# Routing tokens to experts batch by batch during attention, with the experts' token lists written to DRAM by indirect DMAs

## The reference: cross attention, then a mixture of experts

```python
x = x + attention(query=layernorm(x), key=ctx, value=ctx)   # softmax(Q K^T / sqrt(32)) V, then @ Wo.T + bo
flat = layernorm(x).reshape(4096, 512)
logits = flat @ router_weight.T + router_bias               # 8 experts
topk_vals, topk_idx = top_k(softmax(logits), 2)
gate, up = split(flat @ gate_up_proj[e] + gate_up_bias[e])  # per expert e, 512 -> 2 x 512
gate = minimum(gate, 7); up = clip(up, -7, 7)
act = (up + 1) * gate * sigmoid(1.702 * gate)
x = x + sum over the 2 best experts of w_e * (act @ down_proj[e] + down_bias[e])
```

## Time and profile before

| | |
|---|---|
| median of three runs | 1759.33 us (1756.08 to 1760.47) |
| the profiled execution | 1756.44 us, of which the span is 1754.7 us |
| mean granted TensorE clock | 0.965 of full speed |
| TensorE busy | 1617.4 us (92%) |
| VectorE busy | 1246.5 us (71%) |
| GpSimd busy | 801.6 us (46%) |
| ScalarE busy | 659.0 us (38%) |
| attention | until about 971 us |
| routing | 971 to 1019 us |
| experts | 1019 us to the end |

### The profile page before, as it was taken

The page is one execution under the profiler, slowest core; times in us unless marked ns, Lnnn a source line. Parts: engine busy times, 40 slices in busy tenths (PEclk is TensorE's granted clock), DMA queues, the critical chain, the costliest instruction groups (busy, mean ns, idle before and its releaser), DMA issues. The chain is left out here.

```text
span 1754.7 us, 30046 instructions
## 1 busy us (share of the span) xinstructions
PE 1617.4 (92%) x9637; PEld 1189.2 (68%) x9637; DVE 1246.5 (71%) x2223; ACT 659.0 (38%) x1265; POOL 801.6 (46%) x619
## 2 busy tenths in 40 slices
PE   5889999999999999999987269999999999999995
PEld 3545555555565655556533269999999998999994
DVE  4675777777777767776664867777878778777873
ACT  3354544545445354454441033223333233222320
POOL 3364656556565655556564022333343433434332
PEclk9999999999999999999998569999999999999998
DMA  6342343434334334333311421324443353324321
GB/s 215 81 122 66 104 111 83 130 89 110 108 92 113 103 93 120 96 100 95 89 52 60 159 74 62 98 86 159 162 153 115 94 206 112 105 79 148 113 79 66
DMA packets 98804, 188.69 MB, mean 108 GB/s; under 512 B 26320, under 2 KB 27344, under 8 KB 98640
## 3 DMA queue, kind: packets, MB, share of 16 engines
q1 hardware_dynamic: 79408, 123.99, 25.0%
q0 software_dynamic: 19232, 62.73, 11.2%
HBM read 204.19 MB, written 37.36 MB: 138 GB/s over the span
## 5 line engine op out<-in xcount | busy, mean ns | idle before, releaser
L677 DVE TENSOR_REDUCE negmax<-max_ps 128x2 f32<-128x1024 f32 x256 | 312.4, 1220 | 203.7 <-PE max_ps L446 203.4
L566 ACT ACTIVATE pt<-work 128x512 f32<-128x512 f32 x512 | 278.4, 594 | 242.2 <-PE work L458 228.8
L760 POOL TENSOR_TENSOR acc<-acc,pt 128x1024 f32<-128x1024 f32 x128 | 303.8, 2377 | 121.8 <-ACT pt L566 121.8
L1295 PE MATMUL gu_ps<-xgT_hi,wg_hi 128*128 128x256 f32 x1248 | 355.3, 285 | 0.0
L1295 PE MATMUL gu_ps<-xgT_hi,wg_lo 128*128 128x256 f32 x1248 | 352.0, 282 | 0.0
L1295 PE MATMUL gu_ps<-xgT_lo,wg_hi 128*128 128x256 f32 x1248 | 351.8, 282 | 0.0
L757 POOL TENSOR_TENSOR acc<-pt 128x1024 f32<-128x1024 f32 x64 | 152.9, 2391 | 248.9 <-PE work L478 181.1
L1295 PEld LDWEIGHTS gu_ps<-xgT_lo,wg_hi 128*128 128x128 f32 x1248 | 235.8, 189 | 0.1
L1295 PEld LDWEIGHTS gu_ps<-xgT_hi,wg_hi 128*128 128x128 f32 x1248 | 235.7, 189 | 0.1
L1295 PEld LDWEIGHTS gu_ps<-xgT_hi,wg_lo 128*128 128x128 f32 x1248 | 235.6, 189 | 0.0
L1556 POOL DMA_INDIRECT out<-acc,idx x78 | 77.5, 994 | 325.0 <-DVE acc L1450 319.0
(11 more groups left out here) (201 smaller groups left out, 2803.0 us busy)
## 6 DMA issues: line engine op xcount, KB each, us to landing
raw_g<-w_gate_up SPq DMA_DIRECT2D x39, 2048.0 KB
raw_d<-w_down SPq DMA_DIRECT2D x39, 1024.0 KB
ks<-k_hi SPq DMA_DIRECT2D x252, 64.0 KB, 2.0
qs<-q_hi SPq DMA_DIRECT2D x252, 64.0 KB, 2.0
bd<-b_down SPq DMA_DIRECT2D x39, 256.0 KB
x_in<-x SPq DMA_DIRECT2D x32, 256.0 KB, 3.1
ctxT_raw<-ctx_t SPq DMA_DIRECT2D x32, 256.0 KB, 3.9
x<-x SPq DMA_DIRECT2D x32, 256.0 KB, 3.0
```

The lines of the kernel that those rows point to most:

```text
L566: e.activation(pt[k % 2][:, h, :], in_work("exp", u, k, h)[:, :], ACT.Exp, scale=scale).then_inc(exped.sem, 1)
L677: e.tensor_reduce(negmax[:, u % 2, n:n + 2], max_ps[:, :, :], AX.X, ALU.max, negate=True).then_inc(maxed.sem, 1)
L760: e.tensor_tensor(acc[:, heads, :], acc[:, heads, :], pt[k % 2][:, heads, :], ALU.add).then_inc(added.sem, 1)
L1295: ins = e.matmul(gu_ps[n % GU_BANKS][:, part, :], wg[s][pw][:, k, cols], xgT[s][px][:, k, :], start=(k == 0 and m == 0), stop=(k == KD - 1 ...
```

## The change

The routing of a tile no longer waits for all 32.

- The 32 tiles are cut into nine groups: six of the four tiles of a batch, then two of three and one of two. A group's logits, masks and shares stand in one of two halves of small buffers.
- For batches 0 to 5 the group's work has keys in ORDER, in the second to fourth unit of the batch after the next: `best 0` and `best 1` (the two best experts, VectorE) in rounds 2 and 3 of the second unit, `soft` (the exp, ScalarE) in round 4, `share` (VectorE; SP stores the shares) in round 5, `rank` (two accumulating products on TensorE, over the group's masks and the counts of all tiles before it) in round 2 of the third unit, `place` (VectorE) in round 3, and `list` in rounds 2 and 3 of the fourth.
- `list` is new: for each of two experts per token and each tile one indirect DMA of GpSimd writes the 128 token numbers of that tile, 4 bytes each, to their places in a table in DRAM, `token_list`, which has 32 rows of 128 places per expert and 78 spare rows, and is cleared once at the start of the program.
- The last three groups follow at the end: the group of tiles 24 to 26 in step 32, tiles 27 to 29 and 30, 31 in step 33; the four list DMAs of the last group stand in the routing stage.
- The routing stage keeps the counts, the experts of the tiles and these small steps at the end. The one-hot tables and their 64 products are gone. Instead VectorE computes for each of the 78 slots the row of `token_list` where it begins, GpSimd gathers these 78 rows of 512 bytes once all lists have landed, TensorE transposes them, and VectorE copies them.
- Constants (iota, part, tri, ones) are made on GpSimd at the start of the program and turned into floats by VectorE before the first group. The experts' stage waits for nine stores of shares instead of one.

```diff
+def route_groups(n_tiles, batch):
+    last = n_tiles - 2 * batch
+    return [(n, batch) for n in range(0, last, batch)] + [(last, batch - 1), (last + batch - 1, batch - 1), (last + 2 * batch - 2, 2)]
...
+def list_tile(e, token_list, listed, pos, token, n):
+    places = token_list.rearrange("r (q a) -> (r q) a", a=1)
+    for s in range(TOP_K):
+        at = bass.IndirectOffsetOnAxis(ap=pos[:, s, n:n + 1].bitcast(U32), axis=0)
+        e.indirect_dma_start(out=places, out_offset=at, in_=token[:, n:n + 1], in_offset=None).then_inc(listed, 16)
...
+            for r, lag, *keys in ((2, 9, ("best", 0)), (3, 9, ("best", 1)), (4, 9, ("soft",)), (5, 9, ("share",)), (2, 10, ("rank",)), (3, 10, ("place",)),
+                                  (2, 11, ("list", 0), ("list", 1)), (3, 11, ("list", 2), ("list", 3))):
+                g, odd = divmod(s - lag, T)
+                if g in groups[:-3] and not odd:
+                    at(r, *[(kind, g, *what) for kind, *what in keys])
...
+                at(1, ("best", g, 0))
+                at(2, ("best", g, 1), ("soft", g), ("rank", g))
+                at(3, ("place", g))
+                at(4, ("share", g))
+            if s == units[-1] + 2:
+                at(0, *[("list", g, t) for t in range(GROUPS[g][1])])
+                g += 1
+                at(1, ("best", g, 0), ("best", g, 1), ("soft", g))
+                at(2, ("rank", g), ("place", g), *[("list", g, t) for t in range(GROUPS[g][1])])
+                at(3, ("best", g + 1, 0), ("best", g + 1, 1), ("soft", g + 1), ("rank", g + 1), ("share", g), ("place", g + 1), ("share", g + 1))
             if s - 1 in units[:-1]:
                 for t in range(T):
                     at(4 + t, ("norm", s - 1, t))
...
+            def rank_tokens(g):
+                to, slots = take("rank", g), slots_of(g)
+                cols = slice(0, GROUPS[g][1] * E)
+                e.wait_ge(before_made.sem, before_made[g])
+                e.matmul(to[:, cols], tri[:, :], hots[:, slots, :].rearrange("p t e -> p (t e)"), start=True, stop=False)
+                e.matmul(to[:, cols], ones_b[:, :], before[:, slots, :].rearrange("p t e -> p (t e)"), start=False, stop=True).then_inc(ranked.sem, 1)
...
+            def soften(g):
+                e.wait_ge(expo_made.sem, expo_made[g])
+                e.activation(expo[:, slots_of(g), :], expo[:, slots_of(g), :], ACT.Exp).then_inc(softened.sem, 1)
...
+            def best_experts(g, s):
+                slots, n = slots_of(g), GROUPS[g][1]
+                e_of = lambda a: a.unsqueeze(2).to_broadcast([P, n, E])
+                t_of = lambda a: a.unsqueeze(1).to_broadcast([P, n, E])
+                source = masked if s else logits
+                if s == 0:
+                    e.wait_ge(logits_out.sem, logits_out[sum(GROUPS[g]) - 1])
+                last()
+                then(e.tensor_reduce(best[:, s, slots], source[:, slots, :], AX.X, ALU.max))
+                last()
+                then(e.tensor_tensor(scratch[:, slots, :], source[:, slots, :], e_of(best[:, s, slots]), ALU.is_equal))
+                last()
+                then(e.tensor_tensor(scratch[:, slots, :], scratch[:, slots, :], t_of(expert_less[:, :]), ALU.mult))
+                last()
+                then(e.tensor_reduce(pick[:, slots], scratch[:, slots, :], AX.X, ALU.min))
+                last()
+                then(e.tensor_tensor(hot[s][:, slots, :], t_of(expert_less[:, :]), e_of(pick[:, slots]), ALU.is_equal))
+                last()
+                if s == 0:
+                    then(e.scalar_tensor_tensor(out=masked[:, slots, :], in0=hot[0][:, slots, :], scalar=-1e30, in1=logits[:, slots, :],
+                                                op0=ALU.mult, op1=ALU.add))
+                    return
+                then(e.tensor_tensor(hots[:, slots, :], hot[0][:, slots, :], hot[1][:, slots, :], ALU.add))
+                e.tensor_tensor(expo[:, slots, :], logits[:, slots, :], e_of(best[:, 0, slots]), ALU.subtract).then_inc(expo_made.sem, 1)
+                if g and slots.start == 0:
+                    then(e.tensor_copy(before[:, 0, :], before[:, SLOTS, :]))
+                for t in range(slots.start, slots.stop):
+                    last()
+                    ins = e.tensor_tensor(before[:, t + 1, :], before[:, t, :], hots[:, t, :], ALU.add)
...
+            def share(g):
+                slots, n = slots_of(g), GROUPS[g][1]
+                e.wait_ge(softened.sem, softened[g])
+                if g in groups[1:-1]:
+                    e.wait_ge(w_stored, 16 * g)
+                then(e.tensor_reduce(exp_sum[:, slots], expo[:, slots, :], AX.X, ALU.add))
+                then(e.tensor_tensor(weight[:, weights_of(g), :], expo[:, slots, :], hots[:, slots, :], ALU.mult))
+                last()
+                then(e.reciprocal(inv_sum[:, slots], exp_sum[:, slots]))
+                last()
+                e.tensor_tensor(weight[:, weights_of(g), :], weight[:, weights_of(g), :], inv_sum[:, slots].unsqueeze(2).to_broadcast([P, n, E]),
+                                ALU.mult).then_inc(weight_made.sem, 1)
+            def place_tokens(g):
+                slots, n = slots_of(g), GROUPS[g][1]
+                e.wait_ge(ranked.sem, ranked[g])
+                then(e.tensor_tensor(scratch[:, slots, :], in_work("rank", g)[:, 0:n * E].rearrange("p (t e) -> p t e", e=E),
+                                     base[:, :].unsqueeze(1).to_broadcast([P, n, E]), ALU.add))
+                for s in range(TOP_K):
+                    last()
+                    then(e.tensor_tensor(hot[s][:, slots, :], hot[s][:, slots, :], scratch[:, slots, :], ALU.mult))
+                for s in range(TOP_K):
+                    last()
+                    then(e.tensor_reduce(pos_f[:, s, slots], hot[s][:, slots, :], AX.X, ALU.add))
+                last()
+                e.tensor_copy(pos[:, :, tiles_of(g)], pos_f[:, :, slots]).then_inc(pos_made.sem, 1)
             for kind, *what in ORDER:
...
+                elif kind == "list":
+                    g, t = what
+                    if what == [0, 0]:
+                        e.wait_ge(s_cleared, 16)
+                    e.wait_ge(pos_made.sem, pos_made[g])
+                    list_tile(e, token_list, listed, pos, token, GROUPS[g][0] + t)
...
             for kind, *what in ORDER:
                 if kind in "kq" and what[1] == 1:
...
+                elif kind == "share":
+                    g, = what
+                    e.wait_ge(weight_made.sem, weight_made[g])
+                    e.dma_start(w_rows[:, tiles_of(g), :], weight[:, weights_of(g), :]).then_inc(w_stored, 16)
...
-            flat_pos = pos[:, :, :].rearrange("p s t -> p (s t)")
...
-            for q in range(NQ):
...
-                then(e.tensor_tensor(row_hot[:, some, :], iota_b[:, :].unsqueeze(1).to_broadcast([P, n_some, P]),
...
-                then(e.tensor_tensor(col_hot[:, some, 0, :], col_hot[:, some, 1, :],
...
-            e.wait_ge(listed, 1)
-            then(e.tensor_copy(low[:, :], list_ps[:, SLOTS:]))
-            last()
-            then(e.scalar_tensor_tensor(out=token_1[:, :], in0=list_ps[:, 0:SLOTS], scalar=float(P), in1=low[:, :],
-                                        op0=ALU.mult, op1=ALU.add), "token_1")
+            then(e.tensor_scalar(slot_hot[:, :], iota[:, 0:E], slot_expert[:, 0:1], None, ALU.is_equal))
+            last()
+            then(e.tensor_tensor(slot_hot[:, :], slot_hot[:, :], start[:, :], ALU.mult))
+            then(e.scalar_tensor_tensor(out=slot_row[:, :], in0=slot_expert[:, :], scalar=float(NT), in1=part[:, 0:1], op0=ALU.mult, op1=ALU.add))
...
+            then(e.tensor_reduce(slot_start[:, :], slot_hot[:, :], AX.X, ALU.add))
...
+            then(e.scalar_tensor_tensor(out=slot_row[:, :], in0=slot_start[:, :], scalar=-float(SUB), in1=slot_row[:, :], op0=ALU.mult, op1=ALU.add))
+            last()
+            then(e.tensor_copy(row_i[:, :], slot_row[:, :]), "rows")
...
+            e.wait_ge(turned, 1)
+            then(e.tensor_copy(token_1[:, :], list_ps[:, :]), "token_1")
...
-            for n in range(KT):
...
-                ins = e.matmul(list_ps[:, :], row_hot[:, n, :], col_hot[:, n, :, :].rearrange("p a c -> p (a c)"),
-                               start=(n == 0), stop=(n == KT - 1))
-            ins.then_inc(listed, 1)
+            e.matmul(count_ps[:, :], ones_b[:, :], before[:, before.shape[1] - 1, :], start=True, stop=True).then_inc(counted, 1)
+            e.wait_ge(columns_in, 16)
+            e.transpose(list_ps[:, :], columns[:, :], ident[0:SLOTS, 0:SLOTS]).then_inc(turned, 1)
...
+        def on_pool(e):
+            e.memset(ones_e[:, :], 1.0).then_inc(consts_made, 1)
+            e.memset(ones_row[:, :], 1.0).then_inc(consts_made, 1)
+            first_tile, n = groups[-1]
+            for t in range(n):
+                list_tile(e, token_list, listed, pos, token, first_tile + t)
+            e.wait_ge(vec, at["rows"])
```

(3 more changed lines are left out.)

300 lines of the change are left out of this document (137 added, 163 removed).

## The result

| | before | after |
|---|---|---|
| median of four runs | 1759.9 us (1756.08 to 1760.69) | 1811.55 us (1809.31 to 1815.18) |
| ratio after to before, 95% interval | | 1.0301 (1.0285 to 1.0318) |
| profiled execution, span | 1756.44, 1754.7 us | 1809.48, 1807.8 us |
| mean granted TensorE clock | 0.965 | 0.956 |

What follows compares the result with a forecast made beforehand. TensorE, busy 291.80 of 300 us in attention, and the 48.9 us routing hole were taken to bound the kernel. Terms -21 + 27 + 2 + 7 + 6 + 1 = +22 gave a median of 1781 us, range 1752 to 1796.

Steps and rivals of the forecast that it cites:

- VectorE in attention, +27: Second units: new VectorE steps wait out GpSimd's adds on the shared port and delay TensorE; +27 us, bounds 0 and 40.
- Rival (1): Attention: VectorE's bursts slip past GpSimd's adds, so the 27 us fall away; 1754 us, 18% chance.
- Rank, +2: Attention: the ranking's two small matmuls per group take 0.3 us each time on TensorE; +2 us.
- GpSimd in attention, +7: Fourth units: eight scatters delay the add and, through ScalarE's exp, TensorE by 1.4 us in five groups; +7, bounds 4 and 14.
- Last unit, +6 and +1: End of attention: lists end 6.5 us late without slack, +6; logits of tiles 27 to 31 pass between new steps, +1.
- Routing stage, -21: Last logits to first index: first index 21.9 us earlier, 0.9 given back for overlap; -21 us, bounds -26 and -15.
- rival (5): Routing stage: the list's gather lies behind 6.3 MB of weights, landing after 7 us instead of 3; 1785 us, no chance given.
- (4): Rival: 4-byte scatters take longer than row scatters, each 0.25 us more costing 12 in attention, 4 in the stage; 1797, 7%.
- (3): Rival: only each best 1's first add is met, lists cost nothing till the last unit; +4, about 1761 us, 10%.
- A batch takes 6 to 7 us more: Sign in attention: each batch takes 6 to 7 us longer than in the kernel before.
- The exp behind them waits for acc: Sign in the fourth unit: ScalarE's exp behind eight list DMAs, 1.3 us apart, waits for GpSimd's add.
- The hole falls to about 27: Sign: last logits to first index falls from 48.9 to about 27 us; staying above 35 means the forecast is wrong.

Runs made afterwards that it cites:

- split_best: The change with best 1 cut in two, the second half one unit later, and the keys after it moved; 1820.21 us, 1.0364 of the kernel before.
- gap64: The change with the places of the table 64 bytes apart instead of 4, still 4 bytes written to each; 1801.07 us, 1.0267 of the kernel before.
- no_lists: The change without the list scatters and the wait for them, so all experts work on token 0; 1753.14 us, 0.9975 of the kernel before.
- gap64_late: gap64_spread with the six scatters of the last group but one moved behind the end of the attention block; 1775.79 us, 1.0097 of the kernel before.
- full64: The change with places 64 bytes apart and all 64 bytes written by each scatter; 1802.7 us, 1.0266 of the kernel before.
- gap64_spread: gap64 with four scatters of a batch in the fourth unit and four in the next; 1771.06 us, 1.0066 of the kernel before.
- gap16_spread: gap64_spread with places 16 bytes apart instead of 64; 1765.26 us, 1.0042 of the kernel before.
- gap16_split: gap16_spread with best 1 split over two units, lists one unit later and rank right ahead of place; 1750.36 us, 0.9955 of the kernel before.
- gap16_late: gap16_split with six scatters moved behind the attention block's end, and SP waiting for all lists before the weights; 1748.65 us, 0.9944 of the kernel before.
- gap16_drain: gap16_split with GpSimd waiting for the scatters issued so far to land before the attention block ends; 1752.72 us, 0.9962 of the kernel before.
- near_split: gap16_split's order with the change's own table, places 4 bytes apart; 1772.62 us, 1.0084 of the kernel before.

## Why the prediction was wrong, step by step

**What bounds the kernel.** Right. TensorE had no time to give: the last logits come 56.3 us later than before, and that is the sum of what single places lost (46.8 from unit 10 to 31, 12.4 in the tail, less 2.9 at the start); nothing was won back in between.

**VectorE in attention, +27; measured +18.8.** The mechanism was right and shown: the blocked steps end with GpSimd's add, split_best takes the loss to 1.3. Mis-sized was how many groups meet a second add. I took four at 5.5 and two at 2.6; measured are 6.0, 2.0, 2.4, 2.0, 2.2 and 4.2, and only the first is seen to meet one. I had written that the second block is missed if the chain is 0.3 us faster, and took the worse side. Part of the two large ones is the clock, which I had left out. Behind the waits of the first group, TensorE (busy 4.84 of the 7.2 us ahead) was granted 0.50 for 6.8 us:

```profile
315.20:322.00 6.80, 5.81 (x20) 2.90 (x21) 6.60 (x10) 1.61 (x3) 2.35 (x1) 0.50 0.36 88
```

and the sixth group loses 4.2 to 4.3 in the four runs whose clock is at 0.50 for 3.4 us there (the change, gap64, no_lists, gap64_late) and 2.6 in the three without (full64, gap64_spread, gap16_spread). Rival (1), that the bursts slip past the adds, is refuted by the row of 2.03 us. **Rank, +2**: 1.2 with place, right.

**GpSimd in attention, +7; measured +26.8.** This step failed, in what it let the scatters delay. I let the add start 4.7 us late, and it does so by 4.3 in gap64 (737.81 at a lag of 27.7, against 705.85); I let nothing wait but the exponential of 710.68, which does need that add, and brought 1.4 us of it to TensorE. In the runs the loss stands before that exponential, at the maximum of round 4: eight scatters in a row make results of TensorE 3.8 us late for their readers, and gap64 loses 3.4 to 4.8 in each of five batches, gap64_spread nothing. How they do that is open. The remaining 7.8 us (26.8 - 19.0), 6.1 of them in the first batch, go with the q stacks of 13.6 us and the fall of the clock behind them (gap64 has the stacks at 2.0), a price of which the trace of before had no row, and which I did not list among the unknowns: I asked what a scatter costs GpSimd, not what it costs the DMA queues.

**Last unit, +6 and +1; measured +12.4.** I counted 6.5 us of delay, and the first add is 5.9 us late against the other engines (968.49, against 918.83 + 43.8). What I left out is what TensorE does after such a wait. Stretches of the change and of before at the same work:

```profile
965.00:970.00 5.00, 1.42 (x13) 0.58 (x5) 3.33 (x6) 0.00 (x0) 4.37 (x4) 1.00 0.02 0
970.00:975.00 5.00, 3.11 (x4) 1.46 (x5) 0.00 (x0) 2.66 (x5) 5.00 (x3) 0.55 0.81 34
975.00:980.00 5.00, 5.00 (x24) 1.99 (x23) 0.00 (x0) 1.36 (x3) 4.97 (x3) 0.76 0.19 20
```

```profile
921.00:926.00 5.00, 5.00 (x32) 2.23 (x28) 3.15 (x6) 3.73 (x7) 5.00 (x4) 1.00 0.18 54
```

After 3.6 of 5 us without work the granted clock is 0.55 and 0.76 in the next two stretches, so most of the first and about half of the second ran at the lower of its two levels (1.2 GHz), where it had been 1.00 (2.4 GHz). What this costs was not measured by itself. no_lists and gap16_split, in which the wait is gone, have tails of 1.3 and 1.1 (gap16_late and gap16_drain, of the same order, 3.1 and 3.8).

**Routing stage, -21; measured -3.1.** The VectorE part was right: no_lists has a hole of 23.3 us, 25.6 less than before, at my lower bound. What failed is the price of the scatters at the memory: 9.76 us of landing where I took 2.3 (bounds 1.5 and 3.5), and 11.50 at the block's end where I took 0.3. I had taken the landing from a scatter of whole rows, whose places lie 2 KB apart. That row holds only for places that are apart: gap64 measured 2.05. The gather of the rows landed 5.0 us after its issue ended (6.0 after it began) where I took 3.0, beside the weights (2 to 7 was its range, and rival (5) its name). Together the three add 20.7 us to the forecast; the hole is 18.8 longer than forecast, so the rest of it came out 2 shorter. By the Trainium skill (DMA: Bandwidth & Descriptors, Anatomy of one DMA) the fixed cost of 2.0 us would have given 2.0 in place of 2.3; the traces agree for places with a gap (2.05) and not for neighbours (9.76).

**Rivals.** (4), slower scatters, was the right family at 7%, but I priced it as issue time, and the issue took 958 ns in the median, less than a row gather. (5) came half true, with 5.0 between 3 and 7. In (3) I mixed two bases: +4 on the median of 1759.33 is 1763, and 1760 is the profiled run. The Trainium skill's case of a GpSimd DMA that takes 3100 ns beside a VectorE copy (SBUF - State Buffer, A bandwidth-pool intuition that's wrong) did not occur: the longest of 64 issues took 1111 ns.

**What would show it.** "A batch takes 6 to 7 us more": 16 in the first, then 6.2 to 7.5, and that is luck, as VectorE's part is smaller and the scatters' part larger than I took. "The exp behind them waits for acc": it does not. "TensorE waits 3 to 4 us for negmax": the second units lose 2.0 to 6.0. "The hole falls to about 27": 45.8, over the 35 that I had named as the mark of a failed forecast.

## What to carry to other kernels

Do not put a long run of new steps in front of another step on a busy engine: eight scatters in a row cost 19 us over five batches, four and four nothing. When a loss is put down to a wait, look up in the kernel what the instruction waits for, and look for a batch in which it starts before its supposed releaser ends; two times that lie 0.1 us apart are no proof. Give each new DMA three prices, its issue, its landing, and what it does to the transfers beside it, and let the place in memory be like that of the row from which the price is taken. And when small steps are spread over a busy stage, put each where the other user of the port is idle and free each PSUM bank within a round or two: the same steps on the same table cost 47 us up to unit 31 in the change's order and 10 in near_split's.
